# A banded attention kernel: the mask is added to the transposed scores on TensorE, and GpSimd's selects on the exponentials go

## The reference, cut to what matters

```python
x = transpose(mask, (0, 2, 1))                 # mask: the layer norm of x; 256 positions, 64 channels
q, k, v = split(x @ w_in.T + b_in, 3)          # 8 heads of 8 channels
scores = einsum('bqhd,bkhd->bhqk', q, k) / sqrt(8)
band = abs(idx[:, None] - idx[None, :]) <= 64  # idx = arange(256)
scores = where(band, scores, finfo.min)
attn = softmax(scores, axis=-1)
o = einsum('bhqk,bkhd->bqhd', attn, v) ...
out = (relu(o @ w_out.T + b_out) transposed * ctx) @ w_ct + b_ct
```

## Time and profile before

| | |
|---|---|
| median of 3 runs | 362.23 us (362.06 to 362.73) |
| the profiled execution | 362.1 us, of which the traced span is 360.4 us |
| TensorE's granted clock, mean over the span | 0.98 of full speed |
| PE busy | 320.2 us, 89% of the span |
| PEld busy | 252.3 us, 70% |
| DVE busy | 256.2 us, 71% |
| ACT busy | 208.1 us, 58% |
| POOL busy | 192.7 us, 53% |
| DMA, mean | 34 GB/s |

### The profile page before, as it was taken

How to read it: one execution, slowest core, us unless ns; L and a number is a source line. 1 busy time by engine, 2 the same in 40 slices (tenths; PEclk the granted TensorE clock), 3 DMA queues, 4 the chain that set the end, 5 groups by cost and what they waited for, 6 DMA issues and landing times.

```text
span 360.4 us, 7398 instructions
## 1 busy us (share of the span) xinstructions
PE 320.2 (89%) x2258; PEld 252.3 (70%) x2258; DVE 256.2 (71%) x935; ACT 208.1 (58%) x438; POOL 192.7 (53%) x287
## 2 busy tenths in 40 slices
PE   0689999779798898999999999899999999999993
PEld 0467768567576666767777777777777767888892
DVE  5899999999989899988323615576478846661364
ACT  2639888759687695967841341467577865213210
POOL 4757988758767585856602431515152543244733
PEclk9859999999999999999999999999999999999997
DMA  7996000000000000000000000000000000000011
GB/s 220 363 373 227 1 3 3 1 2 3 1 2 0 3 3 1 3 2 2 2 2 0 0 2 0 1 2 0 2 3 0 2 0 3 0 31 15 1 38 37
DMA packets 10150, 12.16 MB, mean 34 GB/s; under 512 B 1920, under 2 KB 8832, under 8 KB 10112
## 3 DMA queue, kind: packets, MB, share of 16 engines
q1 hardware_dynamic: 9536, 11.36, 9.2%
q10 hardware_dynamic: 576, 0.33, 0.4%
HBM read 10.64 MB, written 1.05 MB: 32 GB/s over the span
## 4 chain that ended last, share of the span: by engine, by line
PE 58%; DVE 27%; issue 8%; ACT 3%; POOL 2%; DMA 1%; POOLq 0%; DVEq 0%; SPq 0%; ACTq 0%
DVE masked L1110 10%; PE S L666 6%; PE S L339 5%; PE O L377 4%; PE ST L690 4%; PE S L472 4%; PE ST L361 4%; PE S L608 2%; PE S L536 2%; PE PJ L449 2%; PE PJ L579 2%; PE O L623 2%; PE PJ L310 2%; DVE st L1072 2%; PE XB L597 2%
## 5 line engine op out<-in xcount | busy, mean ns | idle before, releaser
L1110 DVE CUSTOM_DVE_ANT_0 masked<-S,band 128x192 bf16<-128x192 f32 x256 | 79.1, 353 | 8.4 <-PE S L339 7.3
L785 ACT ACTIVATE ex<-ST 128x384 f32<-128x384 f32 x128 | 62.2, 489 | 14.0 <-PE ST L361 13.4
L339 PE MATMUL S<-qk 128*128 128x384 f32 x128 | 53.5, 424 | 10.2 <-DVE mw L1110 8.1
L948 POOL TENSOR_SCALAR rstd<-mv 128x1 f32<-128x1 f32 x40 | 11.8, 294 | 94.2 <-DVE mv L1074 94.0
L960 POOL TENSOR_TENSOR qk<-kp,kmask 128x1024 fp32r<-128x1024 f32 x24 | 46.3, 1934 | 5.0 <-DVE kp L1208 4.9
L361 PE MATMUL ST<-qk 128*128 128x192 f32 x256 | 48.7, 273 | 0.0
L361 PEld LDWEIGHTS ST<-qk 128*128 128x128 f32 x256 | 44.5, 189 | 1.9 <-issue 1.2
L339 PEld LDWEIGHTS S<-qk 128*128 128x128 f32 x128 | 24.8, 195 | 23.3 <-issue 16.1
L1254 DVE TENSOR_REDUCE mw<-S 128x8 f32<-128x512 f32 x32 | 22.0, 687 | 17.9 <-PE S L536 17.8
L751 ACT ACTIVATE hs<-PJ,sb,cols 128x512 fp32r<-128x512 f32 x29 | 22.5, 777 | 20.6 <-PE PJ L311 20.1
L377 PE MATMUL O<-ex,v 128*32 128x192 f32 x512 | 34.2, 338 | 0.0
(11 more groups left out here) (178 smaller groups left out, 757.9 us busy)
## 6 DMA issues: line engine op xcount, KB each, us to landing
w<-in_w SPq DMA_DIRECT2D x2, 1024.0 KB, 10.1
cx<-in_cx SPq DMA_DIRECT2D x1, 1024.0 KB, 7.9
cxT<-in_cxT SPq DMA_DIRECT2D x1, 1024.0 KB, 9.6
up<-in_up SPq DMA_DIRECT2D x1, 1024.0 KB, 10.9
down<-in_down SPq DMA_DIRECT2D x1, 1024.0 KB, 11.8
out<-x SPq DMA_DIRECT2D x8, 128.0 KB, 1.7
x<-in_x SPq DMA_DIRECT2D x1, 768.0 KB, 5.6
vecs<-in_vecs SPq DMA_DIRECT2D x1, 640.0 KB, 8.0
```

Source lines behind the costliest of these rows:

```text
L339: mm(out, r32(qp[:, t % 2, g, b, P * c:P * c + P]), r32(mv_), start=True, stop=True).then_inc(s["pe_s"], 1)
L785: A(ex[:, (n // 2) % 4, 2 * w:2 * w + 2, :], ST[n % 2][:, 0:2 * WIN].rearrange("p (h k) -> p h k", h=2), ACT.Exp, scale=SCALE).then_inc(s[ ...
L1110: last = V.tensor_tensor_reduce(out=masked[:, n % 2, h, :], in0=S[n % 2][:, WIN * h:WIN * h + WIN], in1=band[:, c, :], scale=1.0, scalar=N ...
```

## The change

The second pass gets the band: ahead of its two matmuls TensorE multiplies the identity `identb` (bf16, 128 x 128) with the band of this chunk (bf16, read twice by a broadcast, 384 columns) into the same `ST` bank with `start=True`, and the two matmuls add to it. GpSimd's selects, and the semaphore they signalled with, are taken out, and L377's wait goes to the exponential itself. VectorE makes the bf16 identity once, at the start.

```diff
--- before.py
+++ after.py
@@ -63,6 +63,7 @@
         cxT = sb("cxT", [P, 2, N * E])
         ident = sb("ident", [P, P])
         band = sb("band", [P, 2, WIN], BF16)
+        identb = sb("identb", [P, P], BF16)
         masked = sb("masked", [P, 2, 2, WIN], BF16)
         kmask = sb("kmask", [P, 4])
         cols = sb("cols", [P, 4])
@@ -145,7 +146,7 @@
                  "pe_proj pe_v pe_s pe_mt pe_st pe_pv pe_ot pe_bt pe_out pe_wct pe_bias "
                  "act_hs act_v act_mt act_exp act_o act_bt act_relu act_xh act_sb "
                  "dve_w dve_band dve_ln dve_xn dve_xl dve_mix dve_max dve_rc dve_on dve_x dve_zero "
-                 "pool_var pool_rstd pool_mw dve_y pool_kb pool_sel pool_zero act_kb dve_spread ld_sel "
+                 "pool_var pool_rstd pool_mw dve_y pool_kb pool_zero act_kb dve_spread ld_sel "
                  "f_ln f_rstd f_xn f_sc f_cmp f_sel fp_sT fp_x fa_x fp_up fa_up fp_dn f_dn fp_sc f_x "
                  "g_ln g_rstd g_xn gp_xT ga_xT gp_k ga_hk g_mk gpool_k gp_v ga_v gp_q ga_hq g_lq gp_e ga_q g_q gp_s g_max gp_mt ga_mt "
                  "gp_st ga_ex gp_pv ga_o gp_ot g_rc g_on g_y gp_bt ga_bt gp_out g_x "
@@ -357,9 +358,13 @@
                         pe.wait_ge(s["act_exp"], n - 1)
                     if n < 2:
                         pe.wait_ge(*((s["dve_mix"], 4), (s["act_v"], 1))[n])
+                    if n == 0:
+                        pe.wait_ge(s["dve_band"], 2)
+                    mm(ST[n % 2][:, 0:2 * WIN].rearrange("p (h q) -> p h q", h=2), identb[:, :],
+                       band[:, c:c + 1, :].to_broadcast([P, 2, WIN]), start=True, stop=False)
                     for h in range(2):
                         last = mm(ST[n % 2][:, WIN * h:WIN * h + WIN], r32(kb[:, t % 2, g, 2 * w + h, b, P * c:P * c + P]),
-                                  r32(qp[:, t % 2, g, b, BAND * c:BAND * c + WIN]), start=True, stop=True)
+                                  r32(qp[:, t % 2, g, b, BAND * c:BAND * c + WIN]), start=False, stop=h == 1)
                     last.then_inc(s["pe_st"], 1)
 
 
@@ -368,7 +373,7 @@
                         continue
                     n = UNITS * t + r
                     b, g, c, w = parts(r)
-                    pe.wait_ge(s["pool_sel"], n // 2 + 1)
+                    pe.wait_ge(s["act_exp"], n + 1)
                     pe.wait_ge(s["act_v"], t + 1)
                     if r % 8 == 0 and n >= 8:
                         pe.wait_ge(s["act_o"], n // 8)
@@ -967,23 +972,6 @@
                 t = T_ - 2
                 if l == 13 and 0 <= t < TILES:
                     inv_std(t, "f_ln", 2 * t + 2, "f_rstd")
-                if T_ >= 0:
-                    t, r = place(T_, l, ST_LAG + 1)
-                    if r % 2 == 0 and live(t, r):
-                        n = UNITS * t + r
-                        b, g, c, w = parts(r)
-                        e = ex[:, (n // 2) % 4, :, :]
-                        pool.wait_ge(s["act_exp"], n + 2)
-                        if c == 0:
-                            G.affine_select(out=e[:, :, 0:64], in_=e[:, :, 0:64], compare_op=ALU.is_ge, fill=0.0, base=BAND,
-                                            pattern=[[0, 4], [1, 64]], channel_multiplier=-1)
-                            G.affine_select(out=e[:, :, 64:WIN], in_=e[:, :, 64:WIN], compare_op=ALU.is_ge, fill=0.0, base=0,
-                                            pattern=[[0, 4], [-1, 128]], channel_multiplier=1).then_inc(s["pool_sel"], 1)
-                        else:
-                            G.affine_select(out=e[:, :, 0:128], in_=e[:, :, 0:128], compare_op=ALU.is_ge, fill=0.0, base=0,
-                                            pattern=[[0, 4], [1, 128]], channel_multiplier=-1)
-                            G.affine_select(out=e[:, :, 128:WIN], in_=e[:, :, 128:WIN], compare_op=ALU.is_ge, fill=0.0, base=0,
-                                            pattern=[[0, 4], [-1, 64]], channel_multiplier=1).then_inc(s["pool_sel"], 1)
                 t = T_ + 1
                 if l in KB and 0 <= t < TILES:
                     keys(t, *KB[l])
@@ -1193,6 +1181,7 @@
                 if (T_, l) == (-1, 2):
                     dve.wait_ge(s["ld_small"], 64)
                     V.tensor_copy(band[:, :, :], exf[:, 0:2 * WIN].rearrange("p (c k) -> p c k", c=2)).then_inc(s["dve_band"], 1)
+                    V.tensor_copy(identb[:, :], ident[:, :]).then_inc(s["dve_band"], 1)
                 t = T_ + 1
                 if l - 1 in PROJ and 0 <= t < TILES:
                     n = PROJ[l - 1]
```

## The result

The change makes the kernel slower: 364.23 us median of 4 runs (364.0 to 364.45) against 362.17 us for the kernel before beside it (362.06 to 362.73); the ratio is 1.0054, with a 95% interval from 1.0036 to 1.0071. The profiled executions took spans of 362.5 and 360.4 us, so the 2.1 us to be found in the trace are the 2.1 us of the medians.

The account below looks back on a forecast made before the run. Tiles 3 to 6 were taken as held by DVE, tile 7 and behind by PE. Stretch terms +0.3, +0.6, +1.1, -1.2, -0.4, +1.3, +1.9 gave +3.6 on 362.1 us: 365.7, median 365.8, range 361.4 to 370.5.

Parts of the forecast that it names:

- case A: Whole kernel: PE takes the bound over, as summed; 364 to 368 us, chance 0.5.
- The stalls: DVE beside POOL in tile 4: L1156 loses 1.08 us, L1191 0.42, L1135 0.25; L1169's 0.58 stays.
- L1151's new one: DVE at l = 15: the earlier key copy L960 will rather meet L1151, some 0.4 us, where DVE has slack.
- The matmul's price: Each added matmul on PE: 0.17 us, as L339 of equal width; upper end 0.28, lower end 0.12.
- estimate of 114 ns: Added matmul at 384 columns by the skill's stream rate; 123 matmuls would cost some 6.9 us less; chance 0.05 within B.
- the term for the places where TensorE is the bound late in the stage: Tile 7 and the stretch behind it: PE pays for the added matmuls, 1.3 us and 1.9 us more.
- sum of 3.7 us: Tile 4 before: PE's waits over seven places, as excess over shortest steps, leaving 17.6 us of PE work in 21.3.
- PE's remaining waits: Tiles 4 to 6 after: only the wait before L415 stays, 0.7 us beside 20.3 us of PE work.
- that bound (a load that stands free): Added matmul on PE: if L361's load now stood free, some would be hidden; no less than 0.12 us each.
- B: Rival, chance 0.23: DVE's release worth more (L960 comes off L1169, 363.4 us) or matmul cheaper (359 to 361).
- C: Rival, chance 0.17: waits don't shrink as laid out, 1 us more in each of tiles 1 to 7; 369 to 373.
- D: Rival, chance 0.10: early L960 holds other DVE instructions as long; +0.7 in four tiles, +1.2 in tile 3, about 370.

Follow-up runs that it names:

- The kernels with the copies early and late: Early: kernel before, third key copy at l = 10 instead of 14, 357.22 us; late: changed kernel, first key copy waiting for L1135, 361.77 us.
- the kernel with the late keys: Changed kernel with GpSimd's first key copy (L960 at l = 5) waiting from tile 2 on for VectorE's L1135: 361.77 us, ratio 0.9990 to the kernel before.

## Why the prediction was right, point by point

**Direction and bound.** TensorE took the bound over, as forecast: its waits in tiles 4 to 6 fell from some 4 us to 1.6, DVE's idle time rose to 2.1 to 3.0 us a tile, and tiles 4 to 6 came out at 20.98 and 20.99 where 21.05 stood. The time, 364.23, is 1.6 under the 365.8 named and just inside case A (364 to 368).

**The stalls.** Each of the four was foretold with its fate, and each came so, L1169's included; L1151's new one was put at 0.4 us and is 0.3. The key copy starts 2.0 us earlier against the tile's start (1.3 us ahead of it, where it stood 0.7 behind), not 1.5. The kernels with the copies early and late show the mechanism apart from the change: no instruction was taken out there, and VectorE's records shrank. The Trainium skill (SBUF — State Buffer, SBUF: two separate sides) calls the port pair that the two engines share an exclusive lock that is held for a whole instruction, by VectorE for instructions with two SBUF inputs or in a two-port mode. The traces agree that the stall lasts as long as GpSimd's instruction: VectorE's ends 0.1 to 0.3 us behind it (L1169 at 98.77 us beside an L960 until 98.69, L1156 at 91.08 beside one until 90.79). They agree in which are hit as far as they tell: L1156, L1190, L1191 and L1135 have two SBUF inputs, while L1151 and L1169 have one, and no trace shows the mode in which those ran. L1110, which reads PSUM and one SBUF tensor, kept its mean of 352 to 353 ns in every kernel.

**The matmul's price.** 0.17 us was taken from L339 of the same width; 0.18 is what the steps show where L339 stands ahead. The new matmul does not stand 0.17 us ahead of its successor, as the prediction looked for, but 0.04; the price shows in the whole place only. The prediction's estimate of 114 ns, from the stream rate of the Trainium skill (TensorE: Matmul & The Clock Gate, Back-to-back issue gap), is contradicted by that step.

**The step that was off** is the term for the places where TensorE is the bound late in the stage. Tile 7 was put at +1.3 and the stretch behind it at +1.9; they came to +0.8 and +1.0. That is 1.4 of the 1.5 us between forecast and result. The first cause is shown by the steps, the second is only argued.

The first is how I read PE's own work. I counted as a wait what exceeded the shortest step between the same two lines. Where a line always waits, the shortest step has the wait in it. L412 was such a case: before, in tile 7,

```profile
155.11 0.60 PE L391 MATMUL XB<-ident,osb 128*128 128x128 f32 x4
155.54 0.27 PE L412 MATMUL MT<-ident,sc 128*128 128x128 f32 x1
156.04 0.41 PE L339 MATMUL S<-qk 128*128 128x384 f32 x1 [0.23 <-DVE mw L1110]
```

and in the changed kernel

```profile
155.31 0.60 PE L396 MATMUL XB<-ident,osb 128*128 128x128 f32 x4
155.74 0.27 PE L417 MATMUL MT<-ident,sc 128*128 128x128 f32 x1
155.77 0.42 PE L340 MATMUL S<-qk 128*128 128x384 f32 x1
```

0.93 us had been the shortest seen from L391 to L339; free, it is 0.46. With two smaller ones of 0.16 (L361 to L398 and to L415, for which the prediction names a free step of 0.20, while its sum of 3.7 us has 0.36) this puts PE's work in tiles 3 to 6 before at 16.8 us, not 17.6, and that in tile 7 at 15.4, not 15.9 (with 2.7 and 0.1 more that is the 18.2 measured); the same steps give 19.4 us after, 16 x 0.17 more. The waits that the matmul could fill were larger by as much. In tiles 4 to 6 this error was made good by a second: PE's remaining waits are 1.6 us, where 0.7 was laid out, so that 19.4 + 1.6 gave the forecast's 20.3 + 0.7. That tiles 4 to 6 came out within 0.1 us each is luck to this extent.

The second cause is the price behind tile 7, where no L339 stands ahead. By the stretch, eleven matmuls cost 1.01 us, 0.09 each and not 0.17. It is least where L361 followed L377 directly. Before,

```profile
170.60 0.47 PE L361 MATMUL ST<-qk 128*128 128x192 f32 x2
170.91 0.60 PE L391 MATMUL XB<-ident,osb 128*128 128x128 f32 x4
```

and after:

```profile
171.91 0.34 PE L363 MATMUL ST<-band,identb 128*128 128x384 bf16 x1
171.95 0.50 PE L366 MATMUL ST<-qk 128*128 128x192 f32 x2
172.29 0.60 PE L396 MATMUL XB<-ident,osb 128*128 128x128 f32 x4
```

The two matmuls of L361 took 0.31 us here, against 0.20 behind L339; with the new matmul ahead they take 0.38 in both places. So it costs 0.07 here and 0.18 there, and 0.13 on average at the seven places that are not behind L377. A likely reason is that the load of L361's weights was not hidden there before, and that the new matmul, whose own load is short, now hides it; no run shows this by itself. The prediction had seen that bound (a load that stands free), but had set it at 0.12 and dismissed it for all places alike.

**The rivals.** B named the right lever, the release of L1169, and its size of 0.6 us a tile holds (20.4 against 21.0 where the copy waits; see the kernel with the late keys). It did not come about by itself, since the copy follows L1208 and L1169 closely in every kernel without that wait. C and D did not come. The waits did shrink less than laid out, by 0.9 us a tile, which is C's mechanism in its small form, hidden by the work that I had overstated. Two numbers behind the rivals were off, without moving the forecast. The 95% of VectorE, given for the whole stretch of the attention and used for B, holds for tiles 1 to 6 only (94% by the earlier trace rows); over the whole stretch VectorE's records fill 90% and TensorE's 89%. And D counts 0.7 us in four tiles besides tile 3, where there are three, so its sum is about 369 us and not 370.

## What to carry to other kernels

Instructions that hardly any wait is put down to, on an engine that is half idle, can still hold the kernel: look for instructions of VectorE whose length varies between equal shapes, and at what GpSimd runs beside them. Try first to move GpSimd's long instructions in its own queue, which cost nothing here, before its work is given to an engine that is nearly full: here one number and one wait brought 7 us, where moving the work lost 2. And price an edit by a square of kernels (with and without each half), since the two halves hide each other; and when PE's own work is read from the shortest steps, test whether the shortest one has a wait in it.

## What was not expected of the hardware

A bf16 weight load of 128 x 128 takes 97 ns in the record, half of the 196 of L361's successor in fp32r:

```profile
L363 PEld LDWEIGHTS ST<-band,identb 128*128 128x128 bf16 x128 | 12.4, 97 | 12.8 <-issue 3.9
L366 PEld LDWEIGHTS ST<-qk 128*128 128x128 f32 x256 | 46.6, 196 | 0.4
```

The Trainium skill (TensorE: Matmul & The Clock Gate, Weight-path perf modes — Fast Weight Load (FWL) and DoubleRow) has full loads of 128 columns in other types than fp32 about twice as fast, and the rows agree. Whether the short load mattered for the price of the matmul is open. The steps suggest it for the places behind L377 alone; it was not tried by itself, for instance with an identity in fp32r.
